# Gate and up pieces of the shared experts in scan steps of their own, six of seven batches

## The chip, the cores and the metric

The kernel runs on one core of a Trainium2 chip. The metric is the device time of one execution, in microseconds. A core has five engines that run their own instruction streams side by side and meet only at semaphores: TensorE (PE; its weight loads are listed apart as PEld), VectorE (DVE), ScalarE (ACT), GpSimd (POOL) and SyncE (SP, which here only issues DMAs). PE writes its results to PSUM, eight banks of 128 x 512 floats.

## The reference, cut to what matters

The program computes four layers on x of 8 batches x 512 tokens x 512 channels, all in fp32: a state space scan, a mixture of experts, attention, and the mixture of experts again. Each adds its result to x. The first two are what the change touches.

```python
# scan: per batch, 512 channels d, 16 states n
h[t] = exp(dt[t] * a) * h[t-1] + dt[t] * b[t] * x[t]      # step(h, inp)
y[t] = einsum('bdn,bn->bd', h[t], c[t])
# shared experts, on every token, of 2*352 = 704 hidden columns
shared = silu(hidden_states @ sw_gate) * (hidden_states @ sw_up) @ sw_down
return y + shared                                          # y: routed experts, 64 of them, top 6
```

## The kernel before, in words

The work is written out as one plan, a list of items such as `("scan", k)` or `("sg", 0, q, j)`. Every engine walks the whole list in order and issues its own part of each item; semaphores do the rest. So the plan's order is the order of every engine's queue.

**The scan stage.** Each batch has 32 scan steps, one for 128 channels and two states; 256 steps in all, `scan_plan`. In step k, POOL builds the input of step k+2 (`feed`, L1872), ACT builds exp(dt*a) for two states in PSUM banks 2 to 4 (`decay`, L1720, which answers to the item `scan`), DVE runs two TENSOR_TENSOR_SCANs (L1349) and weighs the second state by c (L1358), POOL weighs the first (`weigh_c`, L1880; in every eighth step DVE does it, L1355). PE then sums the step into a y bank by eight transposing matmuls (`y_sum`, L1004): the sum of step k-1 is the last item of step k. `feed` of step k waits for the sum of step k-5, since the input lies in a ring of five. When a block of channels has had its 8 steps, DVE adds its y to x (`x1`, L1364), two steps behind, and that waits for the block's last sum.

**What lies beside the scan.** Other work is put beside the steps by tables of step numbers. `prepare_track(b)` prepares the scan of batch b beside batch b-1 (soft plus in `soft_ln`, L1700, an Ln on ACT, and `dt_sum`, L1339, on DVE). `quad_track(q)` puts the feed forward layer of the 512 tokens of batch q (a quad) beside batch q+1, and goes on into batch q+2: step numbers of 32 and more are steps 0 and on of the next batch. Within a step, items that take something out of a PSUM bank (`TAKERS`) stand before those that fill one; the items of quad q stand ahead of the ones that prepare batch q+2.

**The shared experts of a quad.** The 704 hidden columns are six pieces, j = 0 to 5, the last of 64 columns. For a piece PE makes the gate half (`sg`, L1054, four fp32 matmuls, listed as eight records) and the up half (`su`, L1075); ACT takes the gate through Silu (`silu`, L1747) into the one buffer `ssg`; DVE multiplies it with the up half (`hid`, L1377; of piece 5, L1381). `silu` of piece j waits for `hid` of piece j-1. For piece 5 `sg` makes both halves abreast (L1061, L1063). The tables `GATES` and `UPS` give the scan step of each piece's halves; `silu` and `hid` come two steps behind.

**The ring of banks.** All these products, with the transposes of the normalised tokens (`turn`, L961, taken by ACT's copy `turned`, L1662) and the Ln results, share PSUM banks 5, 6 and 7 in the plan's order: a product waits until the product three before it has been taken.

**ACT's tables.** Exp, Ln and Silu each need their own table, so an ACT_TABLE_LOAD stands between them; Identity (`apply`, L1636, four tiles of normalised tokens, at step 35 of the next quad) and copies need none.

The diff touches `quad_track` and adds a table; `scan_plan` calls it.

Of the kernel before, what the change touches and what calls it, by code (L numbers as in the profile page):

```python
# [16 lines left out]
BATCH, SEQ, H = 8, 512, 512  # L17
# [44 lines left out]
PICK_AT = (22, 23, 24, 27, 33, 35, 37, 41)  # L62
GATES, UPS = (23, 26, 29, 30, 32, 35), (23, 26, 29, 30, 33, 35)
DOWNS = (40, 41, 43, 51)
TURN_LAG, DT_LAG, SILU_LAG, HID_LAG, SO_LAG = 1, 2, 2, 2, 2
FIRST_DT, FIRST_SOFT = (0, 0), (("soft_exp", 3), ("soft_ln", 4), ("dt_sum", 5), ("dtx", 6))
X1_BEHIND = 2
# [232 lines left out]
def quad_track(q):  # L300

    f = ("F", 0, q)
    for name, at in FRONT:
        yield at, ((name, f) if name in ("stats_a", "stats", "rstd", "apply") else (name, 0, q))
    for c in range(HC):
        yield TURN_F[c], ("turn", f, c)
        yield TURN_F[c] + TURN_LAG, ("turned", f, c)
    if q % 2:
        yield FOLD, ("fold", 0, q // 2)
        yield FOLD + 2, ("folded", 0, q // 2)  # L310
        for n in range(PICKS):
            yield PICK_AT[n], ("pick", 0, q // 2, n)
    for j in range(SC):
        yield GATES[j], ("sg", 0, q, j)
        yield UPS[j], ("su", 0, q, j)
        yield GATES[j] + SILU_LAG, ("silu", 0, q, j)
        yield UPS[j] + HID_LAG, ("hid", 0, q, j)
    for t in range(QT):
        yield DOWNS[t], ("fetch", 0, q, t)
        yield DOWNS[t], ("sd", 0, q, t)  # L320
        yield DOWNS[t] + SO_LAG, ("so", 0, q, t)


def first_steps():
# [15 lines left out]
def scan_plan():  # L340
# [5 lines left out]
    for b in range(BATCH):  # L346
        if b > 0:
            for at, item in prepare_track(b):
                beside[(b - 1) * STEPS + at].append(item)
        if b < BATCH - 1:  # L350
            for at, item in quad_track(b):
                beside[(b + 1) * STEPS + at].append(item)
# [1903 lines left out]
```

## Time and profile before

| what | value |
|---|---|
| median of three runs | 3016.0 us (3014.9 to 3018.98) |
| the profiled execution's own time | 3015.6 us |
| its span, first to last instruction | 3013.8 us |
| scan stage, about | 40 to 1045 us of the span |
| a batch of 32 scan steps | 130.0 us (668.4 to 798.4) |
| busy in that batch: PE, DVE, ACT, POOL | 115.1, 121.3, 85.3, 116.3 us |
| mean granted TensorE clock | 0.956 of full |

All times in the rows are microseconds from the start of the span. A timeline row has the start, the time from the first to the last of its instructions, engine, line, operation, what it writes and reads, the count, and in brackets the engine's idle time before it with what ended it. Instructions of one engine overlap a little at their ends, so a start-to-start distance is shorter than a duration.

### The profile page before, as it was taken

The numbers are of one execution on the slowest core, as the hardware profiler recorded it, in microseconds if no ns is written. First come the engines' busy times: TensorE is split into PE (matmuls) and PEld (weight loads), VectorE is DVE, ScalarE is ACT, GpSimd is POOL, SyncE is SP. The second block draws the span as 40 slices with busy tenths as digits, with TensorE's granted clock in tenths as the row PEclk, the third lists the DMA queues.
The fourth block names the chain that finished last, engine by engine and source line by source line (L and its number), as shares of the span: only waits on it lengthen the run. The fifth ranks groups of instructions, "written<-read, shape, count | busy, mean of one in ns | idle before, by whom it ended". The sixth has DMA issues, their size and how long they took to land.

```text
span 3013.8 us, 37461 instructions
## 1 busy us (share of the span) xinstructions
PE 2720.2 (90%) x13484; PEld 1435.0 (48%) x13484; DVE 1772.6 (59%) x3835; ACT 1281.5 (43%) x2693; POOL 1483.1 (49%) x912
## 2 busy tenths in 40 slices
PE   4668888988889879999969999999899999999998
PEld 3454555545555534433335555555544444444443
DVE  5898999999899952222236666665624444222222
ACT  4657566665756411111127676666712220111111
POOL 5999989988998802222135555554500001121211
PEclk7779999999999889999989999999999999999999
DMA  5454555545554369999940000001135324899997
GB/s 187 153 184 154 185 167 166 187 142 195 166 176 164 131 265 358 396 393 393 392 121 1 29 29 29 29 29 42 64 100 189 118 79 159 308 381 338 359 337 218
DMA packets 168234, 566.13 MB, mean 188 GB/s; under 512 B 22832, under 2 KB 24752, under 8 KB 167536
## 3 DMA queue, kind: packets, MB, share of 16 engines
q1 hardware_dynamic: 149904, 521.65, 47.0%
q0 software_dynamic: 17088, 40.90, 5.9%
q8 instruction: 106, 1.74, 0.2%
q10 hardware_dynamic: 1056, 1.18, 0.1%
q14 instruction: 80, 0.66, 0.1%
HBM read 487.89 MB, written 75.79 MB: 187 GB/s over the span
## 4 chain that ended last, share of the span: by engine, by line
PE 53%; DVE 3%; ACT 2%; POOL 2%; DMA 2%; issue 1%; POOLq 0%; SPq 0%; DVEq 0%; ACTq 0%
PE bank L1151 10%; PE bank L1054 5%; PE bank L1075 5%; PE bank L1177 5%; PE bank L1089 5%; PE bank L1202 5%; PE bank L1259 4%; PE bank L1236 3%; PE bank L1224 2%; PE bank L1248 2%; POOL arena L1970 2%; DMA scratch_y<-arena 2%; PE bank L1134 1%; PE bank L1190 1%; ACT arena L1791 1%
## 5 line engine op out<-in xcount | busy, mean ns | idle before, releaser
L1872 POOL TENSOR_TENSOR arena<-arena 128x1024 f32<-128x1024 f32 x256 | 603.9, 2363 | 55.7 <-PE bank L1004 50.4
L1720 ACT ACTIVATE bank<-arena 128x512 f32<-128x512 f32 x512 | 344.5, 689 | 345.2 <-DVE arena L1349 184.7
L1970 POOL TENSOR_TENSOR arena<-arena 128x2048 f32<-128x2048 f32 (+3 forms) x128 | 296.9, 2323 | 275.0 <-DVE arena L1584 274.9
L1004 PE MATMUL bank<-arena 128*128 128x128 f32 x2048 | 296.7, 299 | 104.7 <-POOL arena L1880 103.5
L1791 ACT ACTIVATE arena<-arena 128x256 f32<-128x256 f32 (+3 forms) x512 | 287.1, 565 | 148.6 <-DVE arena L1575 124.9
L1349 DVE TENSOR_TENSOR_SCAN bank<-bank,arena 128x512 f32<-128x512 f32 x288 | 344.7, 1207 | 1.6 <-ACT bank L1720 1.1
L1004 PEld LDWEIGHTS bank<-arena 128*128 128x128 f32 x2048 | 258.0, 154 | 179.7 <-POOL arena L1880 128.5
L1151 PE MATMUL bank<-arena 128*64 128x352 f32 x2048 | 323.8, 470 | 0.0
L1054 PE MATMUL bank<-arena 128*128 128x512 f32 x640 | 298.2, 610 | 18.7 <-DVE arena L1377 18.7
L1075 PE MATMUL bank<-arena 128*128 128x512 f32 x640 | 288.7, 594 | 6.7 <-DVE arena L1339 6.7
L1880 POOL TENSOR_TENSOR arena<-arena 128x512 f32<-128x512 f32 x224 | 286.5, 1279 | 4.7 <-DVE arena L1349 4.5
L1349 DVE TENSOR_TENSOR_SCAN arena<-bank,arena 128x512 f32<-128x512 f32 x224 | 271.8, 1213 | 27.2 <-POOL arena L1872 14.5
L1089 PE MATMUL bank<-arena 128*128 128x512 f32 x640 | 286.5, 599 | 0.0
L1938 POOL DMA_INDIRECT arena<-scratch_xn,arena x64 | 68.7, 1073 | 440.8 <-DVE arena L1543 242.4
L1575 DVE CUSTOM_DVE_ANT_0 arena<-bank,arena 128x256 f32<-128x256 f32 (+3 forms) x512 | 220.9, 487 | 23.7 <-PE bank L1224 15.8
L1151 PEld LDWEIGHTS bank<-arena 128*64 128x64 f32 x2048 | 143.5, 139 | 147.6 <-issue 143.6
L1516 DVE TENSOR_TENSOR arena<-arena,bank 128x352 f32<-128x352 f32 x64 | 33.3, 521 | 306.9 <-issue 178.6
L1377 DVE TENSOR_TENSOR arena<-arena,bank 128x512 f32<-128x512 f32 x80 | 54.7, 683 | 244.5 <-PE bank L1075 243.7
L1075 PEld LDWEIGHTS bank<-arena 128*128 128x128 f32 x640 | 120.4, 190 | 160.2 <-issue 144.7
L1780 ACT ACTIVATE arena<-bank,arena 128x512 f32<-128x512 f32 x64 | 44.0, 687 | 346.7 <-PE bank L1177 324.2
L1054 PEld LDWEIGHTS bank<-arena 128*128 128x128 f32 x640 | 119.5, 195 | 149.9 <-issue 128.8
L1765 ACT ACTIVATE arena<-bank 128x352 f32<-128x352 f32 x64 | 29.7, 464 | 374.7 <-PE bank L1151 362.4
(145 smaller groups left out, 4187.9 us busy)
## 6 DMA issues: line engine op xcount, KB each, us to landing
arena<-scratch_bc SPq DMA_DIRECT2D x128, 1024.0 KB, 5.5
arena<-in_w_out SPq DMA_DIRECT2D x128, 768.0 KB, 15.3
arena<-in_w_gate SPq DMA_DIRECT2D x128, 704.0 KB
arena<-in_w_up SPq DMA_DIRECT2D x128, 704.0 KB
scratch_x<-arena SPq DMA_DIRECT2D x16, 1024.0 KB, 4.7
scratch_xn<-arena SPq DMA_DIRECT2D x15, 1024.0 KB, 4.6
arena<-scratch_x SPq DMA_DIRECT2D x44, 256.0 KB, 6.2
arena<-scratch_x SPq DMA_DIRECT2D x8, 1024.0 KB, 7.5
```

The costliest lines, as they stand in the source:

```text
L1004: i = nc.tensor.matmul(y[:, t * P:(t + 1) * P], w[:, n, t * P:(t + 1) * P], p.ident, is_transpose=True, start=False, stop=g == GROUPS - 1 ...
L1054: i = nc.tensor.matmul(out[:, :], f["swg"][:, c, j * P:(j + 1) * P], xnT[:, c, :], start=c == 0, stop=c == HC - 1)
L1075: i = nc.tensor.matmul(out[:, :], f["swu"][:, c, j * P:(j + 1) * P], xnT[:, c, :], start=c == 0, stop=c == HC - 1)
L1089: nc.tensor.matmul(out[:, :], f["shT"][:, j, t * P:(t + 1) * P], f["swd"][:, j, :], start=j == 0, stop=False)
L1151: i = nc.tensor.matmul(bank[1 + w][mine, 0:INTER], f["xeT"][k % 2][:, c, mine], f["ring"][(2 * k + half) % nw][w][:, c, :], start=c == 0, ...
L1349: nc.vector.tensor_tensor_scan(out=banks[n][:, :] if n or both else h[:, n, :], data0=banks[n][:, :], data1=h[:, n, :], initial=0.0, op0=A ...
L1575: nc.vector.tensor_tensor_reduce(out=p.sc[i % NSC][:, 0:width], in0=bank[c][:, 0:width], in1=p.amask[:, SEQ - width:], scale=-SCALE, scala ...
L1720: nc.scalar.activation(bank[p.da_bank(k, n)][:, :], block_of(p.dt, b, c), ACT.Exp, scale=p.alog[:, c, state:state + 1]).then_inc(*p.decaye ...
L1791: nc.scalar.activation(p.pr[n % 2][:, c, OFFSET[t]:OFFSET[t] + width], p.sc[i % NSC][:, 0:width], ACT.Exp, scale=-1.0, bias=p.nb[:, k % 2, ...
L1872: nc.gpsimd.tensor_tensor(out=p.hb[k % HB], in0=over(block_of(p.dtx, b, c), 1, NG), in1=p.bc[k // 2 % NBC][:, 0], op=ALU.mult).then_inc(*p ...
L1880: nc.gpsimd.tensor_tensor(out=h, in0=h, in1=p.bc[k // 2 % NBC][:, 1, 0, :], op=ALU.mult).then_inc(*p.weighted["pool"].up(k))
L1970: nc.gpsimd.tensor_tensor(out=own, in0=own, in1=over(p.rden[:, k % 2, :], 2, width), op=ALU.mult).then_inc(*p.divided.up(k))
```

## The change

Two tables replace `GATES` and `UPS` for quads 0 to 5. In them no piece has both halves in one step, except piece 5, whose halves one item makes; so between any two halves PE has at least one `y_sum`. Quad 6, the last that lies beside the scan, keeps the old tables. The steps of `sd` (`DOWNS`) are the same.

```diff
 GATES, UPS = (23, 26, 29, 30, 32, 35), (23, 26, 29, 30, 33, 35)
 DOWNS = (40, 41, 43, 51)
+APART = ((23, 26, 29, 31, 33, 36), (24, 27, 30, 32, 34, 36), DOWNS)
+SHARED_AT = [APART] * (BATCH - 2) + [(GATES, UPS, DOWNS)]
 TURN_LAG, DT_LAG, SILU_LAG, HID_LAG, SO_LAG = 1, 2, 2, 2, 2
...
+    gates, ups, downs = SHARED_AT[q]
     for j in range(SC):
-        yield GATES[j], ("sg", 0, q, j)
-        yield UPS[j], ("su", 0, q, j)
-        yield GATES[j] + SILU_LAG, ("silu", 0, q, j)
-        yield UPS[j] + HID_LAG, ("hid", 0, q, j)
+        yield gates[j], ("sg", 0, q, j)
+        yield ups[j], ("su", 0, q, j)
+        yield gates[j] + SILU_LAG, ("silu", 0, q, j)
+        yield ups[j] + HID_LAG, ("hid", 0, q, j)
     for t in range(QT):
-        yield DOWNS[t], ("fetch", 0, q, t)
...
```

The `silu` items of pieces 0 to 5 stood at steps 25, 28, 31, 32, 34, 37 and now stand at 25, 28, 31, 33, 35, 38; the `hid` items stood at 25, 28, 31, 32, 35, 37 and now stand at 26, 29, 32, 34, 36, 38. In the changed file each line from here on is 3 further down, so L1054 is L1057 there.

Three places in the queues follow, all of quad 0; the other five quads read alike but for bank numbers. First PE, steps 25 and 26 of the scan: the second half of the sum of step 24, then the halves of piece 1. `ring0_taken_dve` is the semaphore by which DVE gives back a bank of the ring. Before:

```order
L1004 MATMUL bank0<-arena 128x128 [waits weighted_dve]
L1004 MATMUL bank0<-arena 128x128 x3
L1054 MATMUL bank7<-arena 128x512 [waits ring0_taken_dve]
L1054 MATMUL bank7<-arena 128x512 x3
L1075 MATMUL bank5<-arena 128x512 [waits ring0_taken_dve]
L1075 MATMUL bank5<-arena 128x512 x3
```

Now:

```order
L1007 MATMUL bank0<-arena 128x128 [waits weighted_dve]
L1007 MATMUL bank0<-arena 128x128 x3
L1057 MATMUL bank7<-arena 128x512 [waits ring0_taken_dve]
L1057 MATMUL bank7<-arena 128x512 x3
L1007 MATMUL bank1<-arena 128x128 [waits weighted_pool]
L1007 MATMUL bank1<-arena 128x128 x3
L1007 MATMUL bank1<-arena 128x128 [waits weighted_dve]
L1007 MATMUL bank1<-arena 128x128 x3
L1078 MATMUL bank5<-arena 128x512 [waits ring0_taken_dve]
L1078 MATMUL bank5<-arena 128x512 x3
```

The sum of step 25 moved between the halves. The gate half of piece 1 still takes bank 7, which held the up half of piece 0: it waits for `hid` of piece 0, and that item moved from step 25 to step 26 on DVE.

Second ACT, steps 34 to 36: `silu` of piece 4 (L1747, L1750 in the change) and the four `apply` tiles (L1636, L1639 there), between the decays (L1720, L1723 there). Before:

```order
L1747 ACT_TABLE_LOAD [waits ring0_taken_dve]
L1747 ACTIVATE arena<-bank6 128x512 [waits ring0_made]
L1720 ACT_TABLE_LOAD
L1720 ACTIVATE bank4<-arena 128x512 [waits weighted_dve]
L1720 ACTIVATE bank2<-arena 128x512 [waits scanned]
L1636 ACTIVATE arena<-arena 128x512 [waits rstd_made]
L1636 ACTIVATE arena<-arena 128x512 x3
L1720 ACTIVATE bank3<-arena 128x512 [waits weighted_dve]
```

Now:

```order
L1723 ACTIVATE bank4<-arena 128x512 [waits weighted_dve]
L1723 ACTIVATE bank2<-arena 128x512 [waits scanned]
L1750 ACT_TABLE_LOAD [waits ring0_taken_dve]
L1750 ACTIVATE arena<-bank6 128x512 [waits ring0_made]
L1639 ACTIVATE arena<-arena 128x512 [waits rstd_made]
L1639 ACTIVATE arena<-arena 128x512 x3
L1723 ACT_TABLE_LOAD
L1723 ACTIVATE bank3<-arena 128x512 [waits weighted_dve]
```

The Silu moved behind the decays of step 35, directly ahead of the `apply` tiles, and the table for Exp is loaded behind these.

Third ACT, steps 37 to 39: `silu` of piece 5 and the copies of the transposes (L1662, L1665 in the change). Before:

```order
L1747 ACT_TABLE_LOAD [waits ring0_taken_dve]
L1747 ACTIVATE arena<-bank5 64x512 [waits ring0_made]
L1720 ACT_TABLE_LOAD
L1720 ACTIVATE bank4<-arena 128x512 [waits weighted_dve]
L1720 ACTIVATE bank2<-arena 128x512 [waits scanned]
L1662 COPY arena<-bank7 128x512 [waits ring0_made]
L1662 COPY arena<-bank5 128x512 [waits ring0_made]
L1662 COPY arena<-bank6 128x512 [waits ring0_made]
L1720 ACTIVATE bank3<-arena 128x512 [waits weighted_dve]
```

Now:

```order
L1723 ACTIVATE bank4<-arena 128x512 [waits weighted_dve]
L1723 ACTIVATE bank2<-arena 128x512 [waits scanned]
L1750 ACT_TABLE_LOAD [waits ring0_taken_dve]
L1750 ACTIVATE arena<-bank5 64x512 [waits ring0_made]
L1665 COPY arena<-bank7 128x512 [waits ring0_made]
L1665 COPY arena<-bank5 128x512 [waits ring0_made]
L1665 COPY arena<-bank6 128x512 [waits ring0_made]
L1723 ACT_TABLE_LOAD
L1723 ACTIVATE bank3<-arena 128x512 [waits weighted_dve]
```

The Silu moved behind the decays of step 38, and the table for Exp behind the three copies. The third copy is of the transpose in bank 6, which held the up half of piece 5, so that transpose waits for `hid` of piece 5.

## Rows read from the trace of the kernel before

**Rows 1.** One scan batch: length, busy PE, PEld, DVE, ACT, POOL, clock, DMA share, GB/s.

```profile
668.40:798.40 130.00, 115.07 (x522) 69.54 (x521) 121.25 (x164) 85.28 (x125) 116.29 (x71) 0.96 0.52 172
```

**Rows 2.** Waits of DVE, then POOL, 160 to 1048 us: total, times, longest.

```profile
DVE arena L1364 <- PE bank L1004: 19.3, 7, 4.4
DVE arena L1349 <- ACT bank L1720: 12.4, 13, 2.0
DVE arena L1349 <- POOL arena L1872: 1.9, 1, 1.9
...
POOL arena L1872 <- PE bank L1004: 50.4, 28, 4.2
```

**Rows 3.** Timeline of DVE, steps 26 to 32 of quad 4.

```profile
774.93 1.22 DVE L1349 TENSOR_TENSOR_SCAN arena<-bank,arena 128x512 f32<-128x512 f32 x1 [2.03 <-ACT bank L1720]
...
777.99 1.27 DVE L1339 TENSOR_TENSOR arena<-arena,bank 128x512 f32<-128x512 f32 x2
779.18 1.21 DVE L1349 TENSOR_TENSOR_SCAN arena<-bank,arena 128x512 f32<-128x512 f32 x1
...
782.16 2.34 DVE L1349 TENSOR_TENSOR_SCAN bank<-bank,arena 128x512 f32<-128x512 f32 x2
...
787.57 1.22 DVE L1349 TENSOR_TENSOR_SCAN arena<-bank,arena 128x512 f32<-128x512 f32 x1 [1.30 <-ACT bank L1720]
...
804.51 0.69 DVE L1364 TENSOR_TENSOR arena<-arena,bank 128x512 f32<-128x512 f32 x1 [3.01 <-PE bank L1004]
```

**Rows 4.** Timeline of PE, the same steps and the third transpose of step 37.

```profile
774.03 3.60 PE L1054 MATMUL bank<-arena 128*128 128x512 f32 x8
...
786.32 3.70 PE L1054 MATMUL bank<-arena 128*128 128x512 f32 x8 [1.28 <-DVE arena L1377]
...
799.13 3.60 PE L1075 MATMUL bank<-arena 128*128 128x512 f32 x8
802.57 1.91 PE L1004 MATMUL bank<-arena 128*128 128x128 f32 x16
...
826.22 0.75 PE L961 MATMUL bank<-arena 128*128 128x128 f32 x4 [0.92 <-DVE arena L1381]
```

**Rows 5.** Timeline of ACT, steps 28, 29, 35, 38.

```profile
781.13 1.28 ACT L1747 ACT_TABLE_LOAD   x1
782.43 0.60 ACT L1747 ACTIVATE arena<-bank 128x512 f32<-128x512 f32 x1
...
786.77 2.74 ACT L1720 ACTIVATE bank<-arena 128x512 f32<-128x512 f32 x4
...
814.48 2.94 ACT L1636 ACTIVATE arena<-arena 128x512 f32<-128x512 f32 x4 [0.22 <-POOL arena L1857]
...
829.81 0.60 ACT L1662 COPY arena<-bank 128x512 f32<-128x512 f32 x1
```

**Rows 6.** Timeline of DVE, steps 35 to 38 of quad 4.

```profile
818.35 0.68 DVE L1377 TENSOR_TENSOR arena<-arena,bank 128x512 f32<-128x512 f32 x1
818.95 2.34 DVE L1349 TENSOR_TENSOR_SCAN bank<-bank,arena 128x512 f32<-128x512 f32 x2
...
826.60 1.22 DVE L1349 TENSOR_TENSOR_SCAN arena<-bank,arena 128x512 f32<-128x512 f32 x1 [0.44 <-ACT bank L1720]
```

**Rows 7.** Timeline of DVE, a pick of quad 3 in step 35.

```profile
690.27 0.69 DVE L1451 MAX8 arena<-arena 128x8 f32<-128x512 f32 x1
...
691.67 2.33 DVE L1349 TENSOR_TENSOR_SCAN bank<-bank,arena 128x512 f32<-128x512 f32 x2
```

**Rows 8.** Timeline of PE, piece 1 of quad 3; a product of step 20.

```profile
644.74 5.40 PE L1054 MATMUL bank<-arena 128*128 128x512 f32 x8 [2.72 <-DVE arena L1377]
...
760.10 1.13 PE L984 MATMUL bank<-arena 128*128 128x512 f32 x2 [2.87 <-DVE arena L1392]
```

**Rows 9.** Granted clock behind these two, columns as in Rows 1.

```profile
646.10:649.40 3.30, 3.30 (x5) 1.33 (x4) 3.20 (x6) 2.37 (x4) 3.30 (x3) 0.50 0.75 273
...
760.00:764.00 4.00, 3.90 (x24) 2.85 (x25) 3.81 (x5) 2.87 (x6) 2.64 (x2) 1.00 0.66 181
```

More of the change, by code:

```diff
@@ L312, in quad_track @@
             yield PICK_AT[n], ("pick", 0, q // 2, n)
+    gates, ups, downs = SHARED_AT[q]
     for j in range(SC):
-        yield GATES[j], ("sg", 0, q, j)
-        yield UPS[j], ("su", 0, q, j)
-        yield GATES[j] + SILU_LAG, ("silu", 0, q, j)
-        yield UPS[j] + HID_LAG, ("hid", 0, q, j)
+        yield gates[j], ("sg", 0, q, j)
+        yield ups[j], ("su", 0, q, j)
+        yield gates[j] + SILU_LAG, ("silu", 0, q, j)
+        yield ups[j] + HID_LAG, ("hid", 0, q, j)
     for t in range(QT):
-        yield DOWNS[t], ("fetch", 0, q, t)
-        yield DOWNS[t], ("sd", 0, q, t)
-        yield DOWNS[t] + SO_LAG, ("so", 0, q, t)
+        yield downs[t], ("fetch", 0, q, t)
+        yield downs[t], ("sd", 0, q, t)
+        yield downs[t] + SO_LAG, ("so", 0, q, t)
 def first_steps():
```

## The prediction

> **What bounds the kernel now.** I read the page first, then a table of windows over the scan batches, then the waits of DVE and POOL in the scan stage, and last the timelines of the engines around one quad. The page says little here, since its shares are means over four stages. The change touches the scan stage alone, so that is where to look: in one of its batches DVE is busy 121.25 of 130.00 us, POOL 116.29 and PE 115.07 [rows 1]. DVE is the bound, PE and POOL follow closely. The reader is to see that a microsecond counts there only if it adds to DVE's idle time or takes from it, and there are under 9 us per batch to take.
>
> The waits say what these are. DVE waits 19.3 us in all for PE's sums, always in `x1`, and 12.4 us for ACT's decays [rows 2]. The largest wait in the view is POOL's: 50.4 us in 28 waits for the same sums [rows 2]. It is the one that seems to ask for this change, and it costs nothing by itself, since POOL runs ahead of DVE, which waited for it once, 1.9 us [rows 2]. So the prize is the `x1` wait, 3.01 us at step 32 of quad 4 [rows 3], and one such wait stands behind each of the six quads that the change moves.
>
> **The change part by part.** No instruction is added or removed. PE makes the same halves; what moves is who waits for whom. I take quad 4, an even one, and follow it.
>
> The intended part: ahead of the sum of step 30 PE has now one half less to make, since the gate half of piece 3 comes at step 31 and the up half of it at 32. A half is worth 3.44 us (start to start, 799.13 to 802.57), its record being 3.60 long [rows 4]. With PE's queue never empty that would end the 3.01 us wait. But PE's queue is empty twice.
>
> First wait, step 26. The gate half of piece 1 needs the bank of the up half of piece 0, given back by `hid` of piece 0, and that went from step 25 to 26. In the trace this half starts at 774.03 [rows 4], while DVE idles 2.03 us ahead of the scan of step 26, at 774.93 [rows 3]. Now `hid` stands behind that step's scans, where the soft plus sums stand today (777.99) [rows 3]; it lasts 0.68, so the half starts at 778.67 + 0.06 = 778.73, 4.7 us late, and ends at 782.33. Behind it are queued the sum of step 25, the up half of piece 1 and every sum after. The Silu of piece 1 was free to start at 782.43 [rows 5], so it is not held up. What is left is 0.60 for the `hid` that was hidden in the 2.03 us of idling and now stands in DVE's way (0.68 long, 818.35 to 818.95 start to start [rows 6]): the next scans, at 779.18 and 782.16 [rows 3], and with them ACT, come 0.6 later.
>
> Second wait, step 29, the same with piece 2 and `hid` of piece 1, which leaves step 28. The scan of step 29 waits for its decay, which ran from 786.77 [rows 5]; 0.6 later it starts at 788.17 instead of 787.57 [rows 3]. Its step takes 777.99 - 774.93 = 3.06 up to the place of `hid` [rows 3], so that runs 791.23 to 791.91 and the gate half of piece 2 starts at 791.97 instead of 786.32 [rows 4]. From there PE has three halves and three sums to the end of the sum of step 30. A sum takes (1.91 - 0.17) / 2 = 0.87, and 1.04 to its end [rows 4]: 3 x 3.44 + 2 x 0.87 + 1.04 = 13.10, which gives 805.07. DVE's wait ended at 804.51 [rows 3]. The half that was saved is lost again, and `x1` comes 0.6 later than before.
>
> Third, `hid` of piece 2 goes from step 31, where the `x1` wait hid it, to step 32 behind that wait, and `hid` of piece 3 from 32 to 34: one 0.60 more in DVE's way.
>
> Fourth, step 36. The table load for the Silu of piece 4 waits for `hid` of piece 3, now in step 34. Behind this Silu are queued the four `apply` tiles, then the load of Exp's table, then the decay that DVE needs for step 36. From the end of `hid`: 0.06 to wake, load 1.28, Silu 0.60, tiles 2.94, load 1.28, decay 0.69 (a quarter of 2.74 [rows 5], with its overlap) and 0.11 to DVE (786.77 + 0.69 to 787.57 [rows 3]) make 6.96 [rows 5]. DVE fills of this only step 35, 2.98 as 779.18 to 782.16 [rows 3], less the 0.08 by which instructions overlap: a stall of 4.0. Before, the Silu had gone one step earlier and the tiles ended at 817.42, ahead of DVE's need at 818.95 [rows 5, 6]. In odd quads a pick stands in step 35, 691.67 - 690.27 = 1.40 [rows 7], and the stall is 2.6.
>
> Fifth, step 39. The third transpose of step 37 waits for `hid` of piece 5, now in step 38. ACT's third copy waits for this transpose, Exp's table for the copy, DVE for the decay: 0.06 + transpose 0.75 [rows 4] + 0.15 to ACT (that wake-up is an estimate, from the 0.06 and the 0.11 above) + copy 0.60 + load 1.28 + decay 0.69 + 0.11 [rows 5] = 3.64, against a DVE that is ready 0.08 before `hid` ends: 3.7. What goes is the stall of 0.44 at 826.60 [rows 6], in even quads.
>
> The load is 1.28 long and its Silu starts 0.02 behind it [rows 5]; a change of table costs 1.30. The Trainium skill, ScalarE: Activation LUTs, section What ACT_TABLE_LOAD costs, adds a drain of about 1.38 us to each change of table, 2.66 in all. By that each of the three changes in the fourth and fifth stall would cost 1.38 more, 25 us over six quads. The sum goes by the row.
>
> Sum without TensorE's clock: even quads 0.6 + 0.6 + 4.0 + 3.7 - 0.4 = 8.5, odd quads 0.6 + 0.6 + 2.6 + 3.7 = 7.5; three of each make 48 us.
>
> **TensorE's clock.** Behind an idle 2.72 us PE made a half of quad 3 in 5.40 instead of 3.60 [rows 4, 8], and the granted clock was 0.50 of full there, the 1.2 GHz level, [rows 9]. Now PE idles longer at both waits: 778.73 less the end of the sum of step 24 (774.03 + 0.16) is 4.5. The one of step 29 begins four items behind 778.73, two halves' worth and three sums (778.73 + 2 x 3.44 + 2 x 0.87 + 1.04 = 788.39), and is 3.6. At the first, 1.80 more puts the half's end at 784.13, and the Silu, ready at 783.03 with DVE's 0.6, is held up 1.1, and the scan of step 29 with it. At the second, the 1.80 go straight into `x1`. The bounds are nothing (the clock stays) and 2.9 per quad, 17 in all; below nothing I see no way, since an idle engine is not clocked up for it. I take the first in all six quads and the second in four, as the second idle time is nearer to the one in the rows: 6.6 + 7.2 = 14.
>
> So 48 + 14 = 62 on the profiled execution's own 3015.6, or on the median of 3016.0, the same within the sum's rounding: 3078. The other engines don't give it back: DVE has no idle time in steps 39 to 54 to shrink, and POOL, delayed by the same amount, keeps its place to DVE.
>
> **The rivals.** *The clock stays up*: 3016 + 48 = 3064. For it: behind an idle 2.87 us the clock was 1.00 [rows 8, 9], so a drop is no certainty near that length. Against: both new ones are longer than any in the rows.
>
> *The two ACT stalls are covered*: DVE would have to find its decays made ahead. Then only steps 26 to 32 cost, 6 x 1.2 + 14 = 21, so 3037. For it: ACT is busy only 85.28 of 130.00 us [rows 1]. Against: its queue is in order and there are three banks for decays, so it can't be more than a step and a half ahead, and the load of the table is fixed behind the copies.
>
> *The relief works*, the one on the other side: PE is so far behind DVE at step 26 that `hid` of piece 0 is never what it waits for; then the half less ahead of the sum of step 30 takes out the `x1` waits, 19.3 [rows 2], and 3016 - 19 = 2997 with the ACT stalls covered as well. It decides at PE being 4.7 us later at step 26 than it is. Against: PE started that half at 774.03 without having waited [rows 4], and the bank is freed 4.7 later now.
>
> **How the numbers follow.** Forecast 0.60 (3078), clock stays 0.20 (3064), ACT covered 0.09 (3037), relief 0.05 (2997), and 0.06 for what none of these tells, half of it gains and losses that cancel. About 0.2%, 6 us, is what a measurement of this kernel can tell from no change. Faster 0.05, within it 0.03, slower 0.92. The forecast's own range is 3062 to 3090, upward for a clock that stays low longer, with more than one half at the low level. The range given, 3050 to 3096, also holds the clock rival and its errors of a microsecond per stall.
>
> **What would show it.** Right: in each of the six quads DVE idles some 4.0 or 2.6 us ahead of the scan of step 36 and 3.7 ahead of that of step 39, both released by ACT's decay; PE waits 3.5 us or more ahead of the gate halves of pieces 1 and 2, released by `hid`; the `x1` waits are still there, 3 to 5 us; the clock in the scan batches is below 0.96. Wrong: `x1` waits gone, or stalls of ACT under a microsecond, or a time below 3050.

## The result and the profile after

| kernel | median | runs | span of the profiled execution | granted clock |
|---|---|---|---|---|
| before | 3015.87 us | 4, 3014.9 to 3018.98 | 3013.8 us | 0.956 |
| changed | 3087.24 us | 4, 3085.82 to 3087.95 | 3085.8 us | 0.941 |

The ratio is 1.0234, 95% interval 1.0219 to 1.0250: the change costs 71 us. The forecast was 3078, in a range of 3050 to 3096.

First the scan batch of quad 3, as it answers to [rows 1]: length, busy PE, PEld, DVE, ACT, POOL, clock, DMA share, GB/s.

```profile
707.50:850.60 143.10, 121.18 (x521) 72.29 (x520) 121.90 (x163) 85.36 (x126) 117.46 (x71) 0.90 0.48 156
```

The batch is 143.10 us long instead of 130.00. DVE is busy 121.90 instead of 121.25, ACT and POOL hardly more either: the work is the same, and the 13 us are idle time of the engine that bounds the stage. PE alone is busier, by 6 us, with the clock down from 0.96 to 0.90: the same matmuls at a lower clock.

The waits of DVE between 160 and 1120 us, as [rows 2] (engine, what waits, for what: total, times, longest):

```profile
DVE arena L1352 <- ACT bank L1723: 59.1, 27, 4.4
DVE arena L1367 <- PE bank L1007: 22.0, 7, 3.6
DVE bank L1352 <- ACT bank L1723: 20.7, 7, 3.9
```

The wait that the change takes aim at is still there, 22.0 us in place of 19.3. What is new is DVE waiting for ACT's decays: two rows, 79.8 us together, in place of 13.5 (the 12.4 of [rows 2] and one wait of 1.1 with a bank in front). Both scans of a step appear, since at step 36 the first scan writes to a bank.

The timeline of DVE in quad 4, as [rows 3] and [rows 6]: start, time, engine, line, operation, count, and in brackets the idle time ahead of it.

```profile
823.03 1.22 DVE L1352 TENSOR_TENSOR_SCAN arena<-bank,arena 128x512 f32<-128x512 f32 x1 [3.08 <-ACT bank L1723]
...
826.08 0.68 DVE L1380 TENSOR_TENSOR arena<-arena,bank 128x512 f32<-128x512 f32 x1
...
838.72 1.22 DVE L1352 TENSOR_TENSOR_SCAN arena<-bank,arena 128x512 f32<-128x512 f32 x1 [4.35 <-ACT bank L1723]
...
841.71 0.68 DVE L1380 TENSOR_TENSOR arena<-arena,bank 128x512 f32<-128x512 f32 x1
...
850.58 1.22 DVE L1352 TENSOR_TENSOR_SCAN arena<-bank,arena 128x512 f32<-128x512 f32 x1 [0.97 <-ACT bank L1723]
...
857.37 0.69 DVE L1367 TENSOR_TENSOR arena<-arena,bank 128x512 f32<-128x512 f32 x1 [3.64 <-PE bank L1007]
...
868.23 0.68 DVE L1380 TENSOR_TENSOR arena<-arena,bank 128x512 f32<-128x512 f32 x1
...
875.79 2.35 DVE L1352 TENSOR_TENSOR_SCAN bank<-bank,arena 128x512 f32<-128x512 f32 x2 [3.91 <-ACT bank L1723]
...
885.97 0.69 DVE L1384 TENSOR_TENSOR arena<-arena,bank 64x512 f32<-64x512 f32 x1
...
890.57 1.22 DVE L1352 TENSOR_TENSOR_SCAN arena<-bank,arena 128x512 f32<-128x512 f32 x1 [3.91 <-ACT bank L1723]
```

The bracketed rows are steps 26, 29, 32 (first its scan, then `x1`), 36 and 39; the four rows without a bracket are `hid` of pieces 0, 1, 3 and 5. The 3.91 ahead of steps 36 and 39 did not exist before: DVE waited for nothing there, and 0.44 ahead of step 38 [rows 6]. The wait of step 29 went from 1.30 to 4.35. Step 32 has two: `x1` waits 3.64 instead of 3.01, and its scan had waited 0.97 where it waited for nothing.

ACT shows how the two stalls of 3.91 come about. Its timeline in steps 35 to 39, as [rows 5]:

```profile
868.98 1.28 ACT L1750 ACT_TABLE_LOAD   x1 [1.86 <-DVE arena L1380]
870.28 0.60 ACT L1750 ACTIVATE arena<-bank 128x512 f32<-128x512 f32 x1
870.77 2.92 ACT L1639 ACTIVATE arena<-arena 128x512 f32<-128x512 f32 x4
873.71 1.28 ACT L1723 ACT_TABLE_LOAD   x1
875.00 1.91 ACT L1723 ACTIVATE bank<-arena 128x512 f32<-128x512 f32 x3
...
887.88 0.59 ACT L1665 COPY arena<-bank 128x512 f32<-128x512 f32 x1 [2.41 <-PE bank L964]
888.49 1.28 ACT L1723 ACT_TABLE_LOAD   x1
889.78 1.30 ACT L1723 ACTIVATE bank<-arena 128x512 f32<-128x512 f32 x2
```

Read it from DVE's `hid` of piece 3, which ends at 868.91: the table load wakes at 868.98, the Silu follows, then the four `apply` tiles, Exp's table, and at 875.00 the decay that DVE has been waiting for, whose scan starts at 875.79. In ACT's queue each of these begins where the one ahead of it ends. At step 39 `hid` of piece 5 ends at 886.66, PE's third transpose runs from 886.72 (1.13 long, forecast as 0.75), the third copy is done at 888.47, the table at 889.77. In both stalls a load is 1.28 long and what needs it starts 0.02 or 0.01 behind, 1.30 per change of table. The Trainium skill's drain of about 1.38 us for each change (ScalarE: Activation LUTs, What ACT_TABLE_LOAD costs) doesn't show in these rows; with it the three changes would have made the two stalls 4.1 us longer together.

PE has two waits per quad, as [rows 4] and [rows 8]. These are the gate halves of piece 1 in quads 0, 2, 4 and 5, with that of piece 2 behind it in quads 0 and 4:

```profile
258.33 5.96 PE L1057 MATMUL bank<-arena 128*128 128x512 f32 x8 [6.61 <-DVE arena L1380]
273.18 5.37 PE L1057 MATMUL bank<-arena 128*128 128x512 f32 x8 [2.84 <-DVE arena L1380]
...
542.56 5.40 PE L1057 MATMUL bank<-arena 128*128 128x512 f32 x8 [4.52 <-DVE arena L1380]
...
826.81 6.73 PE L1057 MATMUL bank<-arena 128*128 128x512 f32 x8 [3.31 <-DVE arena L1380]
...
842.44 5.40 PE L1057 MATMUL bank<-arena 128*128 128x512 f32 x8 [2.84 <-DVE arena L1380]
...
969.23 5.50 PE L1057 MATMUL bank<-arena 128*128 128x512 f32 x8 [6.75 <-DVE arena L1380]
```

Such a half took 3.60 with PE's queue full [rows 4]. Here all twelve behind a wait, the six not shown among them, took 5.1 to 6.7. The clock of the two halves of quad 4, columns as in [rows 1]:

```profile
826.20:832.90 6.70, 6.09 (x7) 2.52 (x8) 6.67 (x8) 2.67 (x3) 6.70 (x5) 0.50 0.39 138
...
843.30:846.50 3.20, 3.20 (x5) 1.34 (x4) 3.10 (x4) 1.74 (x2) 3.11 (x3) 0.50 0.92 294
```

Both stretches are at 0.50 of full, the 1.2 GHz level. The first half ends at 833.54, so it was at that level for all but its last 0.6 us at most.

**Where the 71 us are.** I added up every idle time of DVE of 0.25 us or more in the six quads' steps: 34.8 us before, 103.4 now. The difference, 68.6, is nearly all of it. The spans differ by 72.0, and all of that lies in the scan stage; the other 3.4 are not idle time: from the first scan of batch 1 to the last of the stage DVE is busy 841.8 us, where it was 838.3. Of this, 2.0 are one operation of the router on 256 columns (L1423, L1426 in the change), which takes 1.14 us on average instead of 0.86. No run shows why.

| quad | 0 | 1 | 2 | 3 | 4 | 5 | sum |
|---|---|---|---|---|---|---|---|
| DVE's idle time, after less before | 11.8 | 10.5 | 11.0 | 12.2 | 13.1 | 10.1 | 68.7 |
| of it ahead of step 36 | 3.90 | 2.52 | 3.92 | 2.87 | 3.91 | 2.52 | 19.6 |
| of it ahead of step 39, less 0.44 in even quads | 3.5 | 3.9 | 3.5 | 3.9 | 3.5 | 3.9 | 22.1 |
| what is left, steps 26 to 32 | 4.4 | 4.1 | 3.6 | 5.4 | 5.7 | 3.7 | 26.9 |

### The profile page after: what moved, and what is told of

Read it like the earlier page. It is cut to its first block, busy times and chain, and to the rows that moved or that the text cites. A ratio compares the mean times of both kernels' runs of the same rounds, so it can differ in the third digit from the quotient of the medians.

```text
span 3085.8 us, 37461 instructions
## 1 busy us (share of the span) xinstructions
PE 2745.6 (89%) x13484; PEld 1447.1 (47%) x13484; DVE 1776.2 (58%) x3835; ACT 1282.1 (42%) x2693; POOL 1484.3 (48%) x912
## 4 chain that ended last, share of the span: by engine, by line
PE 52%; DVE 3%; ACT 2%; POOL 2%; DMA 1%; issue 1%; POOLq 0%; SPq 0%; DVEq 0%; ACTq 0%
PE bank L1154 10%; PE bank L1180 5%; PE bank L1057 5%; PE bank L1078 5%; PE bank L1092 5%; PE bank L1205 5%; PE bank L1262 3%; PE bank L1239 3%; PE bank L1227 2%; PE bank L1251 2%; POOL arena L1973 2%; PE bank L1137 1%; PE bank L1193 1%; ACT arena L1794 1%; PE bank L1064 1%
## 5 line engine op out<-in xcount | busy, mean ns | idle before, releaser
L1723 ACT ACTIVATE bank<-arena 128x512 f32<-128x512 f32 x512 | 343.8, 688 | 331.0 <-DVE arena L1352 180.9
L1057 PE MATMUL bank<-arena 128*128 128x512 f32 x640 | 314.0, 637 | 50.1 <-DVE arena L1380 50.1
L1352 DVE TENSOR_TENSOR_SCAN bank<-bank,arena 128x512 f32<-128x512 f32 x288 | 344.8, 1207 | 21.2 <-ACT bank L1723 20.7
L1007 PEld LDWEIGHTS bank<-arena 128*128 128x128 f32 x2048 | 262.7, 156 | 181.1 <-POOL arena L1883 115.7
L1078 PE MATMUL bank<-arena 128*128 128x512 f32 x640 | 287.8, 592 | 0.0
L1092 PE MATMUL bank<-arena 128*128 128x512 f32 x640 | 286.6, 599 | 0.0
L1941 POOL DMA_INDIRECT arena<-scratch_xn,arena x64 | 68.7, 1074 | 442.8 <-DVE arena L1546 244.2
L1057 PEld LDWEIGHTS bank<-arena 128*128 128x128 f32 x640 | 125.6, 205 | 191.4 <-issue 138.5
L1361 DVE TENSOR_TENSOR arena<-bank,arena 128x512 f32<-128x512 f32 x256 | 176.6, 690 | 14.5
```

The costliest lines, as they stand in the source:

```text
L1007: i = nc.tensor.matmul(y[:, t * P:(t + 1) * P], w[:, n, t * P:(t + 1) * P], p.ident, is_transpose=True, start=False, stop=g == GROUPS - 1 ...
L1057: i = nc.tensor.matmul(out[:, :], f["swg"][:, c, j * P:(j + 1) * P], xnT[:, c, :], start=c == 0, stop=c == HC - 1)
L1078: i = nc.tensor.matmul(out[:, :], f["swu"][:, c, j * P:(j + 1) * P], xnT[:, c, :], start=c == 0, stop=c == HC - 1)
L1092: nc.tensor.matmul(out[:, :], f["shT"][:, j, t * P:(t + 1) * P], f["swd"][:, j, :], start=j == 0, stop=False)
L1352: nc.vector.tensor_tensor_scan(out=banks[n][:, :] if n or both else h[:, n, :], data0=banks[n][:, :], data1=h[:, n, :], initial=0.0, op0=A ...
L1723: nc.scalar.activation(bank[p.da_bank(k, n)][:, :], block_of(p.dt, b, c), ACT.Exp, scale=p.alog[:, c, state:state + 1]).then_inc(*p.decaye ...
```

## The experiments

In the change the takers (`silu`, `hid`) follow from the tables of halves by a fixed lag of two steps. The first theory is that of the prediction, that the takers' new steps cost the time and the halves' new steps don't. The rival is that the order of PE's halves and sums does. So in all kernels below but two the takers' steps are written out, apart from the halves'.

**e1: the new order of the halves, all takers early.** Nothing but the takers' steps differs from the changed kernel:

```diff
-APART = ((23, 26, 29, 31, 33, 36), (24, 27, 30, 32, 34, 36), DOWNS)
+APART = ((23, 26, 29, 31, 33, 36), (24, 27, 30, 32, 34, 36),    # halves, as in the change
+         (25, 28, 31, 33, 34, 37), (25, 28, 31, 33, 35, 37))    # silu, hid
...
-        yield gates[j] + SILU_LAG, ("silu", 0, q, j)
-        yield ups[j] + HID_LAG, ("hid", 0, q, j)
+        yield silus[j], ("silu", 0, q, j)
+        yield hids[j], ("hid", 0, q, j)
```

> PE's order of the changed kernel, with silu of pieces 0 to 5 at steps 25, 28, 31, 33, 34, 37 and hid at 25, 28, 31, 33, 35, 37: hid of every piece one step behind its up half. Theory (the cost is in the takers' steps, not in the sums between the halves): every stall of DVE ahead of steps 36 and 39 goes, the x1 waits go too (the sum of step 30 would end near 800.1 in the time of the kernel before, x1 wants it at 801.5), so about 3016 - 19 = 2997, below both kernels. Rival (PE's new order costs by itself: sums between halves, more idle time, lower clock): still above 3016, 3030 or more.

Measured: 2998.91 us (2997.06 to 3001.41), ratio to before 0.9948, interval 0.9931 to 0.9965. The rival falls: with the order of the change and the takers early the kernel is 86 us faster than the changed one by the ratios, and 0.5% faster than before. (Early means the steps of the kernel before, but for piece 3: its up half is made in step 32 now, so its takers are in step 33, not 32.) DVE's waits from 160 to 1030 us:

```profile
DVE arena L1353 <- ACT bank L1724: 10.5, 13, 2.0
DVE arena L1381 <- PE bank L1079: 3.0, 3, 1.9
DVE arena L1368 <- PE bank L1008: 2.5, 5, 1.4
```

The `x1` wait (here L1368) is 2.5 us in place of 19.3 [rows 2], and the new waits for ACT are gone. DVE's idle time, added up as above, is 18.8 us, where the kernel before has 34.8. This is the best of all the kernels that ran.

**e2 and e3: one half of the takers early.** In e2 `hid` of pieces 0, 1 and 2 is early and the end late; in e3 the other way round, with the Silu of pieces 4 and 5 early too.

```diff
+         (25, 28, 31, 33, 35, 38), (25, 28, 31, 34, 36, 38))    # e2: silu, hid
+         (25, 28, 31, 33, 34, 37), (26, 29, 32, 33, 35, 37))    # e3: silu, hid
```

> PE's order of the changed kernel, hid of pieces 0, 1, 2 early (25, 28, 31), pieces 3 to 5 as in the changed kernel (silu 33, 35, 38, hid 34, 36, 38). Theory: the stalls ahead of steps 36 and 39 stay as they are, 19.6 and 23.5 us in all, the wait of PE at steps 26 and 29 and the x1 waits go: 2997 + 42 + 4 for a hid in the open = 3043. Rival (the stalls at 36 and 39 are only the backlog of the late steps 26 and 29 passed on): they go as well, about 3000.

> PE's order of the changed kernel, hid of pieces 0 to 2 as in the changed kernel (26, 29, 32), silu 33, 34, 37 and hid 33, 35, 37 for pieces 3 to 5. Theory: the stalls ahead of steps 36 and 39 go (3.3 and 3.9 us a quad), the late step 26 and 29 and the x1 waits of 3.64 us stay: 3087 - 42 = 3045. Rival (the two parts overlap, one hides behind the other): within 15 us of the changed kernel.

Measured: e2 3042.17 us, ratio 1.0096 (1.0079 to 1.0112); e3 3041.39 us, ratio 1.0094 (1.0077 to 1.0111). Each lies where it was expected within 4 us. The waits of DVE, same stretch, e2:

```profile
DVE arena L1353 <- ACT bank L1724: 32.8, 17, 3.9
DVE bank L1353 <- ACT bank L1724: 20.7, 7, 3.9
...
DVE arena L1368 <- PE bank L1008: 3.0, 6, 1.4
```

and e3:

```profile
DVE arena L1353 <- ACT bank L1724: 35.8, 24, 4.2
DVE arena L1368 <- PE bank L1008: 22.0, 7, 3.6
```

The two sets of waits come apart. With the late end, the scans that wait with a bank in front of them cost 20.7, 7 times 3.9 at most; with the late head the `x1` wait is 22.0 to the digit of the changed kernel. By the ratios, which take each kernel against the runs of before on its own chip, the head costs 1.46% (e3 over e1) or 1.38% (the changed kernel over e2), 42 to 44 us, and the end 1.48 or 1.40%, 42 to 45 us. The two add up, and so does DVE's idle time: 103.4 us in the changed kernel, 61.1 in e2, 60.5 in e3, 18.8 in e1. The end's price is the 41.7 of its two rows in the table above; the head's is the 26.9 left there and the 16 us by which e1 is faster than before.

**e4: only the takers of piece 5 early.** This takes the stall of step 39 alone.

```diff
+         (25, 28, 31, 33, 35, 37), (26, 29, 32, 34, 36, 37))    # e4: silu, hid
```

> The changed kernel with silu and hid of piece 5 at step 37 instead of 38, no other change. Theory: the stall of 3.9 us ahead of step 39 goes in all six quads, the one ahead of step 36 stays, 0.4 us comes back ahead of step 38 in some: 3087 - 22 = 3065. Rival (DVE would wait at step 39 anyway, for the third transpose, the copy and the table): no more than 5 us gained.

Measured: 3060.64 us, ratio 1.0156 (1.0136 to 1.0177), 0.78% or 23.5 us below the changed kernel's, 4 us under what was expected. Six times 3.91 is the same 23.5; the intervals leave the difference uncertain by some 8 us, so that it agrees so closely is luck. DVE's waits:

```profile
DVE arena L1353 <- ACT bank L1724: 33.8, 24, 3.5
DVE arena L1368 <- PE bank L1008: 21.4, 7, 3.6
DVE bank L1353 <- ACT bank L1724: 20.7, 7, 3.9
```

Against the changed kernel's 55.2, 22.0 and 20.7 in the same stretch, only the first has moved, by 21.4 (five of the six stalls lie ahead of 1030 us, 19.6). The stall of step 39 is the one that has gone; that of step 36 (20.7) stands whole.

**c1: the clock kept up in the two waits of PE.** The changed kernel, with 40 and 24 transposing matmuls of a tile of zeros, added to a y bank, ahead of the gate halves of pieces 1 and 2. They add nothing to the sums, and PE makes them while it would wait.

```diff
+    def keep_busy(b, c, n):
+        for i in range(n):
+            nc.tensor.matmul(bank[Y_BANKS[c % 2]][:, i % QT * P:(i % QT + 1) * P], p.nil, p.ident,
+                             is_transpose=True, start=False, stop=False, skip_group_check=True)
...
+        if m == 0 and q < BATCH - 2 and j in (1, 2):
+            keep_busy(q + 1, 2 if j == 1 else 3, 40 if j == 1 else 24)
```

> The changed kernel, and ahead of the gate halves of pieces 1 and 2 of quads 0 to 5 PE makes 40 and 24 transposing matmuls of a tile of zeros, added to an open y bank (they change nothing): 4.4 and 2.6 us of work in the time in which it only waited for hid. Theory (the part of the loss beyond 48 us is TensorE at its 1.2 GHz level behind the two waits, 71 - 48 = 23): the halves take 3.6 instead of 5.3 us and more, the granted clock of the scan batches goes up, time 3087 - 23 = 3064. Rival (the waits themselves are longer than worked out, the clock is not what costs): 3080 or more.

Measured: 3073.28 us, but spread over 3063.03 to 3075.53; ratio 1.0181 (1.0155 to 1.0206). The median is 12 us below the changed kernel on the same chip (3085.41), by the ratios 15, which the two intervals leave uncertain by some 9. The expected 3064 has a ratio of 1.0157, at the lower end of the interval; the rival's 3080 has 1.0210, above it. PE's timeline, piece 1 in quads 0 and 1, piece 2 in quad 2, and pieces 1 and 2 of quad 4:

```profile
258.61 5.40 PE L1065 MATMUL bank<-arena 128*128 128x512 f32 x8 [2.21 <-DVE arena L1388]
...
398.38 5.40 PE L1065 MATMUL bank<-arena 128*128 128x512 f32 x8 [2.38 <-DVE arena L1388]
...
551.48 3.70 PE L1065 MATMUL bank<-arena 128*128 128x512 f32 x8 [0.25 <-DVE arena L1388]
...
815.65 3.70 PE L1065 MATMUL bank<-arena 128*128 128x512 f32 x8 [0.17 <-DVE arena L1388]
...
828.82 3.70 PE L1065 MATMUL bank<-arena 128*128 128x512 f32 x8 [0.80 <-DVE arena L1388]
```

and DVE in quad 4, steps 26, 29 and 32:

```profile
811.86 1.22 DVE L1360 TENSOR_TENSOR_SCAN arena<-bank,arena 128x512 f32<-128x512 f32 x1 [2.63 <-ACT bank L1731]
...
825.10 1.22 DVE L1360 TENSOR_TENSOR_SCAN arena<-bank,arena 128x512 f32<-128x512 f32 x1 [1.90 <-ACT bank L1731]
...
842.05 0.69 DVE L1375 TENSOR_TENSOR arena<-arena,bank 128x512 f32<-128x512 f32 x1 [3.01 <-PE bank L1008]
```

With both halves at 3.70 the waits of quad 4 are 2.63, 1.90 and 3.01 us, where the changed kernel had 3.08, 4.35, 0.97 and 3.64: 4.5 us less. Over six quads DVE idles 18 us less in the profiled execution, whose span is 16 below the changed kernel's. So the clock is part of the cost. The experiment doesn't take all of it away, since the first half of quads 0 and 1 was still made in 5.40. There DVE's wait ahead of step 29 is 3.02 and 1.63 us, where it is 1.90 and 0.51 in the other even and odd quads: 1.12 more each time, the price that the prediction had for such a half (1.1). With these two, DVE's rows put the clock at 20 us.

**d1: the old order, the takers late.** The fourth corner: halves as before the change, takers at the change's steps.

```diff
-APART = ((23, 26, 29, 31, 33, 36), (24, 27, 30, 32, 34, 36), DOWNS)
+APART = ((23, 26, 29, 30, 32, 35), (23, 26, 29, 30, 33, 35),    # halves, as before
+         (25, 28, 31, 33, 35, 38), (26, 29, 32, 34, 36, 38))    # silu, hid
```

> PE's halves in the steps of the kernel before (GATES, UPS unchanged), but silu and hid in the steps of the changed kernel (25, 28, 31, 33, 35, 38 and 26, 29, 32, 34, 36, 38). Theory (all of the loss is in the takers' steps, and the sums between the halves gain 3 us a quad whatever the takers do): slower than the changed kernel by about one half ahead of the sum of step 30, 3.44 us in six quads: 3087 + 20 = 3107. Rival (late takers do harm only together with PE's new order): between 3014 and 3060.

Measured: 3116.57 us, ratio 1.0332 (1.0315 to 1.0349), 10 us above what was expected. DVE's waits:

```profile
DVE arena L1353 <- ACT bank L1724: 52.3, 24, 3.9
DVE arena L1368 <- PE bank L1008: 51.1, 12, 7.1
```

The two `x1` waits of quad 4:

```profile
878.90 0.69 DVE L1368 TENSOR_TENSOR arena<-arena,bank 128x512 f32<-128x512 f32 x1 [7.08 <-PE bank L1008]
...
884.86 0.69 DVE L1368 TENSOR_TENSOR arena<-arena,bank 128x512 f32<-128x512 f32 x1 [1.68 <-PE bank L1008]
```

The first, at step 32, is the changed kernel's 3.64 and the 3.44 of one half, as expected. The second, at step 33, was not in the expectation and accounts for the 10 us: it is 1.68 or 1.69 in each of the six quads. The gate half of piece 4 needs a bank that `hid` of piece 2 now gives back only at step 32; PE waits 1.38 us for it, starts it at 880.25, and the sum that the second `x1` needs stands behind it in PE's queue.

Ratios to the kernel before, each against its runs on the same chip:

| | takers early | takers late |
|---|---|---|
| halves as before | 1 (before) | 1.0332 (d1) |
| halves apart | 0.9948 (e1) | 1.0234 (the change), 1.0231 (r1, again) |

Putting the halves apart gains in either column, 0.5% or 16 us with early takers and 1.0% or 30 us with late ones: in d1 the `x1` wait is 51.1, in the changed kernel 22.0. Late takers cost 3.3% or 100 us in the one row and 2.9% or 86 in the other. Piece 3 blurs the left column a little, since its takers are a step later in e1 than before.

**d2: e1 with `hid` of piece 0 late.** Does one late taker cost what the first wait of the changed kernel does?

```diff
+         (25, 28, 31, 33, 34, 37), (26, 28, 31, 33, 35, 37))    # d2: silu, hid
```

> The kernel with all takers early (2999), and only hid of piece 0 at step 26 instead of 25. Theory: PE starts the gate half of piece 1 4.7 us late and at the low clock, the half of piece 2 some 4 to 5.7 us late, and the sum of step 30 ends 3 to 4 us after x1 wants it; with 0.6 for hid in the open and up to 2 of ACT held up at step 28: 3 to 5 us a quad, 2999 + 24 = 3023. Rival (one late taker is made good by the slack of PE before step 30): 2999 to 3005.

Measured: 3011.52 us (ten runs), ratio 0.9988 (0.9979 to 0.9998). One late `hid` costs 12 us over e1, half of what I had expected. DVE's waits, and PE's first row, from 160 to 1030 us:

```profile
DVE arena L1381 <- PE bank L1079: 12.2, 6, 2.7
DVE arena L1353 <- ACT bank L1724: 12.0, 10, 2.6
DVE arena L1368 <- PE bank L1008: 3.7, 7, 0.6
```

```profile
PE bank L1058 <- DVE arena L1381: 36.5, 6, 7.2
```

PE does wait in all six quads, up to 7.2 us, and the delay reaches DVE at once: `hid` of piece 1, now in step 28, waits for its up half, 12.2 us in place of 3.0. But at `x1` only 1.2 more is left than in e1. The 9.2 at `hid` of piece 1, the 1.2 at `x1` and 1.5 more at the decays are the 12; what else PE was late is caught up between them. In the changed kernel a second wait begins there; that the head's price is far over this 12 fits that, but no run had the second wait alone.

**r1: the changed kernel a second time.**

> The changed kernel, unchanged, beside the others on the same chip: 3087 within 4 us, as before.

Measured: 3085.41 us, ratio 1.0231 (1.0214 to 1.0248), the first result within 2 us.

## Why the prediction was right, and where a size was off

*The direction and the main terms.* Both stalls of ACT were there in every quad, released by the decay as forecast: ahead of step 36 19.6 us in all for 4.0 and 2.6 per quad (19.8), ahead of step 39 23.5 for 3.7 each (22.2). e3 took both away and e4 the second, and the time with them. The table loads, priced by the row at 1.30, came out at that.

*First and second wait.* PE's waits were forecast as 4.5 and 3.6 us. They are 3.3 to 6.8 and 2.84. `hid` released them, as forecast, but the sign that the prediction named, 3.5 us or more at both, was missed at every second wait and at the first of quad 4 (3.31). The 3.6 was worked out with the first half at full clock. A slow one delays PE by all that it loses, and `hid` of piece 1 by 0.7 less, since ACT had that much to spare, so the second wait shrinks. In c1, where quad 4's first half took 3.70, PE's sums end at 825.41 and the next gate half starts at 828.82: 3.4, near the forecast. Why the first wait differs so much between quads was not followed up. The claim that the saved half is lost again held: the sum of step 30 did not come sooner, `x1` waited 3.64 (3.01). Without the loss of clock, as quad 4 in c1 has it, steps 26 to 32 have 7.54 us of idle time against 6.34 before: the 1.2 per quad of the sum.

*The clock, the term that was mis-sized.* It was put at 14 us: 1.1 behind the first wait in six quads and 1.8 behind the second in four. How a slow first half gets to DVE was right, as the 1.12 of c1 shows; how many halves are slow, and how slow, was not. All twelve halves behind a wait were slow. In the first, the half took 5.40 to 6.73, not 5.40 throughout: 15.0 us above 3.60 in six quads, and less the 0.7 that ACT had to spare each time, 10.8 instead of 6.6. In the second they took 5.13 to 5.40, 10.3 above in all instead of 7.2. Together 21.1. DVE's rows give 26.9 less six times 1.2, 19.7, since one such loss was there before: in quad 1 of the kernel before, the half of piece 2 took 5.26, and `x1` waited 4.4, the longest of [rows 2], where it waits 3.01 in quad 4 [rows 3]. The other terms, 48 in the forecast, came out at 48.9 (19.6, 22.1 and six times 1.2), which with 19.7 is the 68.6 summed. So of the 10.0 us between the forecast of 62 and the 72.0 of the profiled spans, 5.7 are the clock, 0.9 the other terms, and 3.4 the time for which DVE was busy longer, a term that the prediction did not have. The 1.8 of the second wait did not go straight into `x1` alone: part of it became the wait of 0.7 to 0.97 at the scan of step 32, whose decay stands behind the Silu of piece 2. The chain from the slow half to that scan had no place in the working.

*The rivals.* "The clock stays up", 3064: it doesn't, and c1, which keeps it up in ten of the twelve halves, comes to 3073 (3064 lies in its interval). "ACT covered", 3037: e3 is that kernel, with the stalls taken out by hand, and it runs in 3041; so the price was right and the condition was not met. "The relief works", 2997: it named the condition, that `hid` of piece 0 isn't what PE waits for, and e1, which makes it so, runs in 2999 with an `x1` wait of 2.5 us.

*What stays open.* c1's rows of DVE bear out the 20 us put down to the clock, but its times give 12 by the medians and 16 by the profiled spans, and 2 more for its two slow halves; the spread of its runs is too wide to say whether something else was lost. No experiment has the second wait of PE alone, or stops the stall of step 36 alone.

## What to carry to other kernels

In this kernel the step table that sets when work is produced also sets, by a lag, when it is taken. Moving the halves alone gave 0.5%, where moving them with their takers cost 2.3%; so look for such a lag before moving a step. In a ring of banks the taker's place decides when the third product after it can begin, so a product moved later should keep its taker where it was unless the data aren't there yet. On an engine with tables, look at what stands behind the operation that now waits: here the four tiles and the second table load behind one Silu were 4.2 of the 6.9 us.

## What the runs showed of the hardware

The granted clock doesn't follow the length of the idle time alone. In the kernel before, a half behind 2.72 us was made in 5.40 in one quad [rows 8] and another in 3.70, and one behind 0.93 in 5.40:

```profile
253.02 5.40 PE L1054 MATMUL bank<-arena 128*128 128x512 f32 x8 [0.93 <-DVE arena L1377]
...
384.08 3.70 PE L1054 MATMUL bank<-arena 128*128 128x512 f32 x8 [2.72 <-DVE arena L1377]
...
397.10 5.26 PE L1054 MATMUL bank<-arena 128*128 128x512 f32 x8 [2.67 <-DVE arena L1377]
```

Four of the twelve gate halves of pieces 1 and 2 in quads 0 to 5 were slow there, 5.26 to 5.40, and only the last of these rows shows as a longer wait of DVE (the 4.4 above): the three others are of piece 1.

In the changed kernel all six behind 2.84 us were slow, and behind the first wait the longest idle times did not make the slowest halves: 5.50 behind 6.75 us, 6.73 behind 3.31. So the rows of the kernel before told neither how slow a half can get (5.40 at most in these quads) nor which are spared, and the forecast that took 5.40 and two as spared was too low.
